# Tap sums, gate blocks and transposes in another order in a GNN kernel of seven pipelined periods

## The reference

```python
# layer 0
h = relu(bn1(conv1x1(x)));  x_conv = relu(bn2(conv17(h)) + x)       # 17 taps along the nodes
s = x @ w_se.T + b_se;      A = exp(-dist(s, s)) * adj              # s has 3 features
x_nmp = A @ relu(x @ w_msg.T + b_msg)
gi = concat(x_conv, x_nmp) @ w_ih.T + b_ih;  gh = x @ w_hh.T + b_hh
r, z = sigmoid(gi_r + gh_r), sigmoid(gi_z + gh_z);  n = tanh(gi_n + r * gh_n)
x = layernorm(x + (1 - z) * n + z * x)
# layer 1
h = (1 + eps) * x + adj @ x
x = layernorm(x + relu(h @ W1 + b1) @ W2 + b2)
```

## Time and profile before

| | |
|---|---|
| time, 3 runs | 386.90, 387.81, 388.11 us; median 387.81 |
| the profiled execution | 386.43 us, span from first to last instruction 384.5 us |
| mean granted clock of TensorE | 0.989 |
| busy share | PE 94%, DVE 85%, ACT 60%, POOL 58% |

### The profile page before, as it was taken

One profiled execution on the slowest core, in us unless ns is written; L12 is line 12 of the kernel. 1 busy time (PEld: TensorE's weight loads), 2 busy tenths in 40 slices (PEclk: granted clock), 3 DMA queues, 4 the chain that ended last, 5 costly groups with the idle time before them and its releaser, 6 DMA issues.

```text
span 384.5 us, 6418 instructions
## 1 busy us (share of the span) xinstructions
PE 363.2 (94%) x2150; PEld 315.1 (82%) x2150; DVE 326.4 (85%) x669; ACT 232.1 (60%) x435; POOL 222.5 (58%) x195
## 2 busy tenths in 40 slices
PE   3969997999999999999999999999999999999994
PEld 1847876798888998989888898989888998988973
DVE  4999999999699986999689986999879996994584
ACT  4454445664866566673776558574676648555765
POOL 3246273698328763597437963396536983286352
PEclk9996999999999999999999999999999999999999
DMA  7500004030110210120101301130101201000002
GB/s 245 213 0 3 0 0 141 26 112 1 56 55 18 94 40 17 55 111 0 55 5 49 109 0 55 55 108 3 55 1 56 109 3 55 3 0 2 0 29 82
DMA packets 7991, 19.39 MB, mean 50 GB/s; under 512 B 672, under 2 KB 5024, under 8 KB 6944
## 3 DMA queue, kind: packets, MB, share of 16 engines
q1 hardware_dynamic: 7536, 18.50, 13.6%
q10 hardware_dynamic: 432, 0.59, 0.5%
HBM read 14.90 MB, written 4.19 MB: 50 GB/s over the span
## 4 chain that ended last, share of the span: by engine, by line
PE 61%; DVE 30%; issue 5%; DMA 1%; ACT 1%; POOL 1%; SPq 0%; DVEq 0%; ACTq 0%
PE back L1266 26%; PE conv L1266 17%; PE back L1379 6%; DVE stats L1015 3%; PE back L1474 3%; DVE stl L844 3%; DVE tail L1050 2%; PE front L1351 2%; DVE wl L1077 2%; DVE adjT L1120 2%; PE back L1430 2%; DVE sv L865 1%; DVE nmpl L844 1%; DMA tail<-in_conv_dram 1%; PE front L1371 1%
## 5 line engine op out<-in xcount | busy, mean ns | idle before, releaser
L1266 PE MATMUL conv<-sth,wh 128*128 128x256 f32 x217 | 65.4, 301 | 1.9 <-DVE stl L844 1.8
L1266 PE MATMUL conv<-stl,wh 128*128 128x256 f32 x217 | 61.8, 285 | 0.0
L1266 PE MATMUL conv<-sth,wl 128*128 128x256 f32 x217 | 61.7, 284 | 0.0
L538 POOL TENSOR_TENSOR rstd<-rstd,minus_half 128x4 f32<-128x4 f32 (+1 forms) x34 | 38.3, 1127 | 35.3 <-DVE rstd L1019 34.7
L559 POOL TENSOR_TENSOR amat<-amat,adjT 128x512 f32<-128x512 f32 x32 | 50.6, 1609 | 5.4 <-ACT amat L682 5.4
L543 POOL TENSOR_TENSOR xw<-xw,xv 128x512 f32<-128x512 f32 (+1 forms) x17 | 21.4, 1256 | 48.4 <-ACT xw L706 48.4
L1266 PEld LDWEIGHTS conv<-sth,wh 128*128 128x128 f32 x217 | 40.9, 189 | 4.6 <-DVE stl L844 1.7
L1266 PEld LDWEIGHTS conv<-stl,wh 128*128 128x128 f32 x217 | 41.1, 189 | 0.1
L1266 PEld LDWEIGHTS conv<-sth,wl 128*128 128x128 f32 x217 | 40.8, 188 | 0.0
L638 ACT ACTIVATE sth<-sv 128x272 fp32r<-128x272 f32 (+1 forms) x33 | 17.3, 523 | 33.6 <-DVE sv L865 21.5
L567 POOL TENSOR_TENSOR adjT<-adjT,diag 128x256 f32<-128x256 f32 x32 | 28.0, 903 | 8.0 <-DVE diag L1166 8.0
...
## 6 DMA issues: line engine op xcount, KB each, us to landing
...
```

The source lines that it names most:

```text
L538: done(pool.tensor_tensor(rstd[:, k, v, q], rstd[:, k, v, q], minus_half[:, q], ALU.pow), RSTD[k])
L1266: ins = pe.matmul(bank, a, b, start=first and k == 0, stop=last and k == len(todo) - 1)
```

## The change

- PE, steady: both gate blocks of `gb` one behind the other, then MINUS2 and PLUS1, then `factors` and both y transposes in one run, then MINUS1; INF ahead of `aggregate`.
- DVE, steady: `gates` is cut into `reset` and `add_input`; `y_stats` and `y_apply` of both pairs come after the end of y of pair 1, `pair2_sum` and `stream_low(gm, 4)`; one `x_low` ahead of `h_low`, the other behind it; `pair2_add` behind both. ACT: `factors_out` behind `gates(gb, 1)`.
- s = 2 is now written out as well: its HALF and PLUS2 are plain products, and the low parts of the weights of these two points are made in it (`second`). s = 3 to 6 come from the loop.
- Opening: `factors(0)` ahead of `parts1(0)`; token differences of groups 0 and 1 and `first_stream1` on DVE; all four distances of group 0 behind MINUS2; other places for nearly all `tap_high` and `tap_low`, for the low part of x of group 1 (on POOL, in s = 1) and for `x_low(0, 0, 1)`; the plain weights of HALF and PLUS2 in room of their own beside `first_w`, so that s = 2 can still read them.
- `diag` is made by ACT from `ident` and `eps1`. Loads: the weights of messages and of the second layer are two DMAs; x of group 1 waits for x of group 0 alone; one piece of `conv2` and the weights of messages are issued from ACT's queue, `ident` from SP's.
- Small tensors share tiles (`small`, `halfsq` in `stats`), which only makes room. That part of the diff is left out here.

```diff
--- before.py
+++ after.py
+ftaps = first_w[:, NVEC:].rearrange("p (k o) -> p k o", o=P)
+traw = (ftaps[:, 5:10, :], coef[0][:, 1:5, :], ftaps[:, 0:5, :], ataps[:, 5:10, :],
+        gtaps, ataps[:, 0:5, :], coef[3][:, 0:4, :])
...
+W_ORDER = ("conv1", "gates", PLUS1, MINUS2, ZERO, MINUS1, INF, "w1", HALF, PLUS2)
...
     prologue()
     steady(1, 1, True)
+    steady(2, 0, True)
     with eng.Fori(0, (GROUPS - 4) // 2) as i:
-        steady(i * 2 + 2, 0, True)
         steady(i * 2 + 3, 1, True)
-    steady(GROUPS - 2, 0, True)
+        steady(i * 2 + 4, 0, True)
     steady(GROUPS - 1, 1, False)
...
     def prologue():
-        sp.dma_start(first_w[:, :], t["first"]).then_inc(first_loaded, 16)
+        sp.dma_start(first_w[:, 0:NVEC + P], t["first"]).then_inc(first_loaded, 16)
         sp.dma_start(xv[0][:, cols(0)], x_v[0, :, cols(0)]).then_inc(x_pair0_loaded, 16)
+        sp.dma_start(c2raw[:, 0:5, :], t["conv2"][:, 0:5, :]).then_inc(conv2_loaded, 16)
         done(sp.dma_start(xv[0][:, cols(1)], x_v[0, :, cols(1)]), X_LOADED)
-        sp.dma_start(c2raw[:, 0:5, :], t["conv2"][:, 0:5, :]).then_inc(conv2_loaded, 16)
-        sp.dma_start(c2raw[:, 5:9, :], t["conv2"][:, 5:9, :]).then_inc(conv2_loaded, 16)
-        sp.dma_start(later_w[:, :], t["later"]).then_inc(later_loaded, 16)
-        sp.wait_ge(conv2_loaded, 64)
         wait(sp, X_LOADED, 0, 16)
         load_x(1, 1)
+        sp.dma_start(ident, t["consts"]).then_inc(consts_loaded, 16)
+        sp.dma_start(later_w[:, W1_AT:], t["later"][:, W1_AT:]).then_inc(mlp_loaded, 16)
         load_adj(0, 0)
...
-        pool.wait_ge(pads_zeroed, 2)
-        token_diffs(0, 1)
         streams2(0)
-        streams1(0)
-        token_diffs(1)
         for b in range(GB):
             mask(0, 0, b)
         streams2(1)
-        pool.wait_ge(bn_ready, 4)
-        for b in range(GB):
-            add_diagonal(0, 0, b)
-        for h in range(PAIRS):
-            wait(pool, XH_READY, 1, h + 1)
-            done(pool.tensor_tensor(xl[1][:, cols(h)], xv[1][:, cols(h)], full(xh[1][:, cols(h)]), ALU.subtract),
-                 XL_READY)
+        pool.wait_ge(mlp_loaded, 16)
+        pool.wait_ge(diag_ready, 1)
+        wait(pool, NH_READY, 0, 1)
+        add_diagonal(0, 0, 0)
+        add_diagonal(0, 0, 1)
+        wait(pool, MSUM_READY, 1, 1)
+        add_diagonal(0, 0, 2)
+        add_diagonal(0, 0, 3)
     def steady(s, u, front):
         gb, gm = s - 1, s
         streams1(gm)
+        first = isinstance(s, int) and s == 1
         residual(gb, 1 - u, 0)
         residual(gb, 1 - u, 1)
         rsqrt(0, gb, 0)
+        if first:
+            x_low1(0)
...
         act.dma_start(c2raw[:, 13:TAPS, :], t["conv2"][:, 13:TAPS, :]).then_inc(conv2_loaded, 16)
-        act.dma_start(ident, t["consts"]).then_inc(consts_loaded, 16)
+        act.dma_start(c2raw[:, 5:9, :], t["conv2"][:, 5:9, :]).then_inc(conv2_loaded, 16)
+        act.dma_start(later_w[:, 0:W1_AT], t["later"][:, 0:W1_AT]).then_inc(later_loaded, 16)
         act.wait_ge(first_loaded, 16)
...
         act.activation(wh[:, S_GATE:S_GATE + 9, :], graw, ACT.Copy).then_inc(w_high, 1)
-        act.wait_ge(tap_sums, 6)
-        tap_high(HALF)
+        act.wait_ge(consts_loaded, 16)
+        act.wait_ge(eps_ready, 1)
+        act.activation(diag[:, :], ident, ACT.Copy, scale=eps1[:, 0:1]).then_inc(diag_ready, 1)
+        factors_out(0)
         h1_out(1, 0, True)
-        h1_out(1, 1, True)
-        act.wait_ge(bn_ready, 3)
-        factors_out(0)
-        minus2_out(0)
-        tap_high(PLUS2)
         exps(0, 0)
         exps(0, 1)
+        h1_out(1, 1, True)
+        exps(0, 2)
+        exps(0, 3)
+        act.wait_ge(bn_ready, 3)
+        minus2_out(0)
         act.wait_ge(tap_sums, 11)
         tap_high(PLUS1)
-        tap_high(ZERO)
-        exps(0, 2)
-        exps(0, 3)
         minus1_out(0)
         tap_high(MINUS2)
+        nmp_high(0, 0)
+        tap_high(ZERO)
+        xconv_high(0, 0)
         tap_high(MINUS1)
-        nmp_high(0, 0)
-        xconv_high(0, 0)
+        nmp_high(0, 1)
+        xconv_high(0, 1)
+        stream_high(1, 2)
         tap_high(INF)
+        act.wait_ge(mlp_loaded, 16)
         act.activation(w1h[:, :], w1raw, ACT.Copy).then_inc(w_high, 1)
-        xconv_high(0, 1)
-        nmp_high(0, 1)
-        stream_high(1, 2)
+        tap_high(HALF)
+        tap_high(PLUS2)
     def steady(s, u, front):
...
         stream_high(gm, 3)
-        factors_out(gm)
         gates(gb, 1)
         minus2_out(gm)
         stream_high(gm, 4)
+        factors_out(gm)
         if front:
             x_high(gf, 1 - u)
...
-    def first_diffs():
-        wait(dve, H1_READY, 0, 2)
+    def first_diffs(g):
+        wait(dve, H1_READY, g, 2)
+        wait(dve, RI_READY, g - 1, 1)
         done(dve.tensor_tensor(av[:, 0:2, :, :].rearrange("p r b t -> p b r t"), h1[:, :, :, 1, :],
                                h1[:, :, :, 0, :], ALU.subtract), A_DIFF)
+        done(dve.tensor_tensor(av[:, 2:4, :, :].rearrange("p r b t -> p b r t"), one_on(h1[:, :, :, 0, :]),
+                               h1[:, :, :, 1, :], ALU.subtract), A_DIFF)
+    def first_stream1(n, op):
+        wait(dve, PV_READY, 0, 1)
+        done(dve.tensor_tensor(sv[:, ROW[n], :, :], vv[:, 1, :, :], vv[:, 0, :, :], op), R1_READY)
...
         dve.tensor_copy(gbias[:, 3:4], vec[:, BIH + 2:BIH + 3]).then_inc(bn_ready, 1)
-        x_low(0, 0, 1)
+        dve.tensor_scalar(eps1[:, :], vec[:, EPS1:EPS1 + 1], 1.0, None, ALU.add).then_inc(eps_ready, 1)
...
+        half, plus2, minus2, plus1, minus1 = (traw[k] for k in (HALF, PLUS2, MINUS2, PLUS1, MINUS1))
+        even, odd = ataps[:, 10:15, :], utaps[:, 0:5, :]
+        dve.scalar_tensor_tensor(half, w3, 0.5, w2, ALU.mult, ALU.add).then_inc(tap_sums, 1)
         steps[0] += 1
-        taps_step(gtaps[:, 10:15, :], gtaps[:, 10:15, :], 0.5, w1)
-        taps_step(gtaps[:, 10:15, :], gtaps[:, 10:15, :], 0.5, w0)
-        first_diffs()
+        taps_step(half, half, 0.5, w1)
+        taps_step(half, half, 0.5, w0)
+        first_diffs(0)
         half_stream(0)
         zero_stream(0)
         parts2(0)
...
         for k in range(3):
             messages(0, k)
         inf_stream(0)
-        taps_step(utaps[:, 0:5, :], w2, 4.0, w0)
-        taps_step(ataps[:, 5:10, :], w3, 4.0, w1)
-        taps_step(gtaps[:, 5:10, :], ataps[:, 5:10, :], 2.0, utaps[:, 0:5, :])
-        taps_step(ataps[:, 5:10, :], ataps[:, 5:10, :], -2.0, utaps[:, 0:5, :])
+        taps_step(odd, w2, 4.0, w0)
+        taps_step(minus2, w3, 4.0, w1)
+        wait(dve, C1_FULL, 1, 2)
+        taps_step(plus2, minus2, 2.0, odd)
+        taps_step(minus2, minus2, -2.0, odd)
+        factors(0)
         parts1(0)
-        factors(0)
-        taps_step(ataps[:, 10:15, :], w0, 1.0, w2)
-        taps_step(ataps[:, 0:5, :], w1, 1.0, w3)
-        taps_step(gtaps[:, 0:5, :], ataps[:, 10:15, :], 1.0, ataps[:, 0:5, :])
-        taps_step(ataps[:, 0:5, :], ataps[:, 0:5, :], -1.0, ataps[:, 10:15, :])
+        first_stream1(PLUS1, ALU.add)
+        taps_step(even, w0, 1.0, w2)
+        taps_step(minus1, w1, 1.0, w3)
+        taps_step(plus1, even, 1.0, minus1)
+        first_stream1(MINUS1, ALU.subtract)
+        taps_step(minus1, minus1, -1.0, even)
         dve.wait_ge(tap_sums, steps[0])
         u_sum(0, 0)
+        x_low(0, 0, 1)
+        pair2_sum(0)
+        first_diffs(1)
         half_stream(1)
         zero_stream(1)
-        pair2_sum(0)
+        parts2(1)
         pair2_add(0)
-        parts2(1)
         pair1_sum(0)
         pair1_add(0, 0)
         pair1_add(0, 1)
         inf_add(0)
         nmp_low(0, 0)
+        xconv_low(0, 0)
+        nmp_low(0, 1)
         w_low_part(wl[:, S_GATE:S_GATE + 9, :], graw, wh[:, S_GATE:S_GATE + 9, :], w_count("gates"))
-        xconv_low(0, 0)
+        tap_low(PLUS1)
         xconv_low(0, 1)
-        nmp_low(0, 1)
-        tap_low(HALF)
-        tap_low(PLUS2)
-        tap_low(PLUS1)
-        stream_low(1, 2)
-        dve.wait_ge(consts_loaded, 16)
-        dve.scalar_tensor_tensor(diag[:, :], ident, vec[:, EPS1:EPS1 + 1], ident,
-                                 ALU.mult, ALU.add).then_inc(bn_ready, 1)
     def steady(s, u, front):
         gb, gm, gf = s - 1, s, s + 1
-        first = isinstance(s, int) and s == 1
+        first, second = isinstance(s, int) and s == 1, isinstance(s, int) and s == 2
         for k in range(3):
             messages(gm, k)
         factors(gm)
         parts1(gm)
         if first:
-            tap_low(ZERO)
+            stream_low(gm, 2)
+        reset(gb, 0)
+        if first:
             tap_low(MINUS2)
-        gates(gb, 1 - u, 0)
-        if first:
-            tap_low(MINUS1)
+        add_input(gb, 0)
         gates_end(gb, 0)
         stream_low(gm, 3)
-        inf_stream(gm)
-        u_sum(gm, u)
-        gates(gb, 1 - u, 1)
-        y_stats(gb, 0)
+        if first:
+            tap_low(ZERO)
+            reset(gb, 1)
+            tap_low(MINUS1)
+            inf_stream(gm)
```

(63 more changed lines are left out.)

58 lines of the change are left out of this document (33 added, 25 removed).

## The result

The changed kernel takes 393.1 us against 387.4 for the kernel before, a ratio of 1.015 (95% interval 1.012 to 1.019): slower, where 385.1 was forecast, and above the range. Its profiled execution took 393.57 us with a span of 391.8.

What follows compares the result with a forecast made beforehand. PE, busy for 94% of the span, was taken as the bound, with 0.74 us of DVE room per middle period. Opening and first period -5.95, period 2 +2.5, five periods +0.15 each: -2.7, so 385.1 us; range 381.5 to 390.

Steps and rivals of the forecast that it cites:

- the sum for DVE in a middle period: DVE from y(1) to out_sum: free at 217.6 instead of 216.8, out_sum 0.15 us later than 217.50, so +0.15 per period.
- about 0.9: Middle period: time saved because GpSimd masks run partly alone while DVE waits for aggregation, so DVE instructions stretch less in all.
- upper bound on the number caught: Middle period: by the shared-port rule no more DVE instructions can be slowed than POOL has instructions, giving +0.15 per period.
- Rival 1: Middle periods: one more DVE instruction caught by masks or token differences makes DVE the bound, +1.1 each, 389.9 in all; chance 0.23.
- period 7: Last period with the tail: no change, as there is no next group and so no loop; bounds -0.3 and +0.5.
- The opening: Up to the first period's messages: waits -3.5, clock -3.15, distances +0.9, HALF(1) wait +1.0, together -4.75 us.
- the wait at HALF(1): Opening: PE reaches group 1's plain HALF product at 32.3, but half_stream(1) on DVE ends near 33.3, +1.0 us.
- rival 2: Opening: the clock falls there in the new order too, so 3.15 us are not gained, 388.3 in all; chance 0.12.
- The first period: Period s = 1: removed PE stalls less added waits and products, together -1.2 us, bounds -3 and +1.
- The new products: First period: ten plain fp32 records for five taps replace fifteen split ones, twice, +0.4 us of PE time.
- the removed waits: First period: PE stalls gone at T2 and tanh (-2.8), second transpose (-0.6) and PLUS2 (-0.6).
- Period 2: Period 2 alone: tap_low of HALF and PLUS2 ahead of out_sum, +1.5 to +3.6 us, taken as +2.5.

Runs made afterwards that it cites:

- experiment 1: Changed kernel with the old PE, DVE and ACT order in s = 2 to 7; opening, first period and period 2's plain products stay new: 384.6 us, ratio 0.994.
- Experiment 14: Kernel of experiment 1 with half of the columns of each adjacency block left out of GpSimd's masks from group 2 on: 383.2 us, ratio 0.991.
- 10: Changed kernel with half of the columns of each adjacency block left out of GpSimd's masks from group 2 on: 385.7 us, ratio 0.997.
- 15: Changed kernel with the second x_low moved right behind the first, ahead of h_low, in the middle periods: 390.6 us, ratio 1.010.
- experiment 8: Kernel of experiment 1 with the opening's second pair of token differences on GpSimd between its masks instead of on DVE: 385.4 us, ratio 0.997.
- experiment 6: Kernel of experiment 1 with the load of x pair 1 ahead of that of conv2's first five taps: 385.0 us, ratio 0.996.
- 7: Kernel of experiment 1 with period 2's low parts of HALF and PLUS2 weights moved between DVE's reset and add_input: 383.5 us, ratio 0.992.

## Why the prediction was wrong

**The step that failed is the sum for DVE in a middle period, and in it the "about 0.9" of contention that was taken off.** DVE was to be free 0.8 later than before (217.6 instead of 216.8): 0.87 for y_stats(0), 0.1 for the rsqrt and 0.5 to 1.1 of idle time, less the 0.9. Against experiment 1 DVE is free 2.1 later (34.85 us after the messages against 32.74). The idle time before it is 2.38, where experiment 1 has 0.35: 2.03 of the 2.1, near the upper end of the 1.5 to 2.1 that the three added terms give. The contention saved was nil: the six instructions beside GpSimd take 7.58 before with both halves of pair2_add (2.73 + 0.69 + 0.69 + 3.47), and 7.67 after. The masks were to run alone while DVE waits for the aggregation; but they start at 212.74, and of the idle time only the last 0.38 lies behind that. They and a token difference stretched other instructions, not less.

Less the 0.66 that DVE waited for PE there, 1.45 is left, of which 0.98 came through to the period. Experiment 14 shows that the old order wins nothing in periods 3 to 6 from less contention, 10 that the new one is as fast as the old with 2.8 of it less, and 15 that filling 1.32 of idle time gives back 0.6 even with the contention it brings. So the loss needs both: the idle time that came with the order, and the contention that was to shrink and pay for it, and stayed.

By the Trainium skill's page "SBUF — State Buffer", section "SBUF: two separate sides", of a VectorE operation with two SBUF inputs and a GpSimd one that reads SBUF, whichever starts first holds the shared port pair for its whole length and blocks the other. The 1.78 of a sum beside a mask agrees (0.6 of its own and one mask of about 1.2; two undisturbed masks took 2.52 in experiment 8). The forecast used the rule for an upper bound on the number caught, which held, and took a saving that the rule doesn't give.

**Rival 1 came about, by another mechanism.** It had DVE as the bound of every period from 0.6 of delay on, with 389.9 in all. DVE did become the bound of each of them, at 393.1 in all, but by idle time rather than by one more instruction caught (7.58 against 7.67): the transposes ended together, so both blocks' statistics, the normalisation and the wait for aggregation came one behind the other, and y_stats(0) no longer filled the wait for tanh. The chance of 0.23 was too low with all of the 0.74 of room spent in the forecast itself. The same order costs 1.8 in period 7, where 0 was put because the loop isn't there; DVE waits in it 1.67 for ACT's nmp.

**The opening: right signs, the wait at HALF(1) mis-sized.** Factors without a wait, four distances behind MINUS2 with one wait of 0.68, full clock from 28 to 35 (so rival 2 didn't come) all happened. But HALF(1) started at 35.73, not 33.3: x pair 1 behind conv2's taps held the second conv1 product for 1.27 (0.39 to 1.30 with the same code in other runs), put at 0 with a bound of +0.5, and DVE's two operations under the first mask cost 2.2 (in experiment 1 the masks caught the second pair's differences, for 1.4). The 0.8 between these two is the execution's, as the openings under experiment 6 show, and not the change's. Then PLUS2(1) waited 0.69, which the forecast didn't have. Experiment 6 takes the first of these away and gains nothing; in its profiled execution a mask catches DVE's chain. That chain was the term to size: the forecast left it as long as before, but from its first stream row to HALF(1)'s it took 21.6 us (13.37 to 34.95), and 20.8 in experiment 1 (13.16 to 33.96), against 19.7 (12.72 to 32.43, of which the end is in the earlier trace rows).

**The first period** was to shorten by 1.2 and lengthened by 0.15. PE is busy 0.56 more, where +0.4 was put. Of its 4.2 us of idle time 3.8 are left, at other places: 1.10 at the transposes, 0.71 at the aggregation, 0.58 at the MLP, 1.42 at conv1. The new products were sized well; the removed waits were counted in full, and most of them came back elsewhere. That the same DVE work stands behind each is my reading of the rows, not shown by a run.

**Period 2** had +2.5 for two low parts of weights, and took 3.45 more than before, 0.9 of it the new order. The other 2.55 is DVE's again: the output sum started at 131.64, 37.39 after the messages (34.85 in a middle period), right behind the two low parts, which took 3.84 from 127.87 on. That is a little over the 3.6 that the forecast gave as the case in which token differences catch both. In the old order, where DVE has 0.66 of slack to spend, the same low parts cost 1.35 (experiment 1), and 0.5 once they stand in idle time (7).

The median stands 8.0 above the forecast and the span 10.0: the forecast added 1.4 for the profiled execution's distance from the median, which wasn't there in the comparison (before's median is 387.4 in it, and after's profile lies 0.4 above its own median).
